# Seven directions in the projection, sums written over their products, and one more convolution direct

## What is computed

```python
for _ in range(3):                                   # x: 16 images, 64 channels, 64 x 64
    t = relu(conv3x3(x, w1) + b1)
    x = x + (conv3x3(t, w2) + b2) / 3
x = relu(x)
qkv = qkv_w @ x                                      # 8 heads, 8 values each, per pixel
k, v = ln(k), ln(v)                                  # w*(t-mean)/(std(ddof=1)+1e-5)+b, over the 8 values
kv = einsum('bhnd,bhne->bhde', k, v) / N             # 8 x 8 per head
ret = einsum('bhnd,bhde->bhne', q, kv) + x
out = gelu(o2_w @ gelu(o1_w @ ret) + x)
```

## Time and profile before

| | before |
|---|---|
| median of 3 runs | 1303.31 us (1300.70 to 1306.62) |
| the profiled execution | 1304.89 us, span 1303.10 us |
| TensorE busy (matmul) | 1188.0 us, 91% |
| VectorE busy | 1085.5 us, 83% |
| ScalarE busy | 597.4 us, 46% |
| mean granted clock of TensorE | 0.967 |

### The profile page before, as it was taken

The page is one execution under the profiler, slowest core; times in us unless marked ns, Lnnn a source line. Parts: engine busy times, 40 slices in busy tenths (PEclk is TensorE's granted clock), DMA queues, the critical chain, the costliest instruction groups (busy, mean ns, idle before and its releaser), DMA issues. The chain is left out here.

```text
span 1303.1 us, 40508 instructions
## 1 busy us (share of the span) xinstructions
PE 1188.0 (91%) x18613; PEld 805.4 (62%) x18613; DVE 1085.5 (83%) x1425; ACT 597.4 (46%) x642; POOL 91.1 (7%) x119
## 2 busy tenths in 40 slices
PE   6989999999999999999999999999999999785845
PEld 2546766577556766676566875676665875445432
DVE  3658888899888998899988997989978998987563
ACT  0212324454455626544455625554455625544573
POOL 2010110001010100101000100101000110110000
PEclk9989999999999999999999999999999999897876
DMA  7430330315061513515061422515061330430221
GB/s 131 91 68 1 69 68 2 68 36 102 18 150 33 102 36 99 101 36 102 2 164 35 86 52 70 129 35 102 2 163 36 69 69 34 100 68 2 82 51 65
DMA packets 87130, 88.95 MB, mean 68 GB/s; under 512 B 70320, under 2 KB 70320, under 8 KB 86960
## 3 DMA queue, kind: packets, MB, share of 16 engines
q0 software_dynamic: 13824, 51.91, 21.0%
q1 hardware_dynamic: 72496, 33.86, 10.3%
q10 hardware_dynamic: 640, 0.59, 0.3%
HBM read 17.66 MB, written 16.78 MB: 26 GB/s over the span
## 5 line engine op out<-in xcount | busy, mean ns | idle before, releaser
L956 PE MATMUL ps<-xs,w_t 64*64 64x512 f32 x4608 | 519.0, 594 | 10.2 <-DMA xs<-dx 6.3
L982 PE MATMUL ps<-v,fw 64*64 64x256 f32 x6912 | 398.9, 380 | 5.9 <-ACT m L552 4.1
L956 PEld LDWEIGHTS ps<-xs,w_t 64*64 64x64 f32 x4608 | 255.6, 134 | 224.1 <-issue 173.9
L982 PEld LDWEIGHTS ps<-v,fw 64*64 64x64 f32 x6912 | 302.2, 133 | 98.3 <-issue 18.4
L524 ACT ACTIVATE t<-ps,b_col 128x1024 f32<-128x1024 f32 x64 | 72.3, 1129 | 260.4 <-PE ps L956 204.9
L494 POOL DMA_DIRECT2D xs<-dx x96 | 83.4, 965 | 1154.3 <-DVE dx L829 1144.6
L722 DVE TENSOR_TENSOR q<-t 128x2112 f32<-128x2112 f32 x48 | 113.2, 2357 | 28.3 <-ACT t L524 15.4
L989 PE MATMUL ps<-v,sw 64*64 64x256 f32 x2304 | 134.4, 376 | 1.7 <-ACT t L524 1.7
L989 PEld LDWEIGHTS ps<-v,sw 64*64 64x64 f32 x2304 | 116.4, 132 | 21.5 <-issue 10.4
L554 ACT ACTIVATE m<-ps 128x1024 f32<-128x1024 f32 x80 | 82.2, 1028 | 65.6 <-PE ps L982 37.1
L836 DVE TENSOR_REDUCE rstd<-g 128x128 f32<-128x1024 f32 x64 | 77.1, 1216 | 38.7 <-ACT g L606 38.7
(11 more groups left out here) (108 smaller groups left out, 1115.4 us busy)
## 6 DMA issues: line engine op xcount, KB each, us to landing
xs<-dx POOLq DMA_DIRECT2D x96, 528.0 KB, 6.1
xs<-in_x SPq DMA_DIRECT2D x64, 256.0 KB, 5.1
out<-y SPq DMA_DIRECT2D x32, 512.0 KB, 3.1
q<-in_L_conv_w ACTq DMA_DIRECT2D x2, 144.0 KB, 6.1
v<-in_L_conv_w ACTq DMA_DIRECT2D x2, 144.0 KB, 7.3
b_col<-in_L_conv_b ACTq DMA_DIRECT2D x4, 0.2 KB, 6.1
y<-in_L_conv_qkv_w SPq DMA_DIRECT2D x4, 16.0 KB
y<-in_L_conv_o_w SPq DMA_DIRECT2D x4, 16.0 KB
```

The lines of the kernel that those rows point to most:

```text
L956: last = mm(to[CH * side:CH * side + CH, BANK * p:BANK * p + BANK], w1_t[half, tap, :], tile[half, rows, c:c + COLS], start=tap == 0, stop ...
L982: last = mm(to[CH * i:CH * i + CH, at:at + SPAN], fw[rows, product, c, :], from_t[rows, tiles, place, i, c:c + COLS], start=c == 0, stop=c ...
```

## The change

- **Merge.** `sums` is gone and `m` has two buffers, used in turn, with the products ordered so that the first of each couple lie together. VectorE adds the second to the first in place, waits for itself (`summed`), and makes -2 times the second plus the sum in place. The intermediate plane `first` and row 2 come next, then a wait for `halved`, `last` and row 1. ScalarE drains part 0 only after the merge of the half before the previous one.
- **Projection.** The eight values of a head, less their mean, lie in seven dimensions; `kvw` now holds seven orthonormal directions, 112 columns. Drains, squares and reductions handle 896 values where they handled 1024. The maps `k_affine` and `v_affine` turn back; that is more setup in `make_rest`.
- **Last pair.** Half 1 of step 2 of pair 7 is direct: 15 halves of L989 in place of 16.
- **Start.** Chunks are 9, 7, 9 and 7 rows; block 0 needs chunk 0, block 1 chunks 1 and 2, block 3 chunk 3. The first copy of w1 is loaded by SyncE, ahead of x.
- **Order.** All tables are written anew. In the gaps of an iteration, PROJECT 4 to 7 of pairs 0 to 5 move from 11, 14, 17, 19 to 10, 12, 14, 16, RELU 0 and 1 from 16 and 30 to 9 and 23; the merge of the old pair's half 0 of step 1 moves from 9 to 10, behind the new pair's second spread of step 0 (10 to 8); the merge of the new pair's second half moves from 18 to 16, behind PROJECT 7. In iteration 8, PROJECT 1 and 2 of pair 6 are behind gaps 10 and 12, PROJECT 3 behind 16, PROJECT 4 to 7 behind 22 to 26; the first spread of pair 7's last convolution is behind 25 (before: 30), DEVIATION 1 behind 28 (before: 26), OUTER 4 to 7 and the FOLDs behind 31 to 35, the second spread behind 36 (before: 37). In iteration 9, OUTER 0 comes ahead of PROJECT 5 and UP 3 ahead of DOWN 2, and RELU 0 comes behind DEVIATION 1.

```diff
-CHUNK_ROWS = 8
-CHUNKS = ROWS // 2 // CHUNK_ROWS
+CHUNK_ENDS = (0, 9, 16, 25, 32)
+CHUNKS = len(CHUNK_ENDS) - 1
...
-SHORT = ({(1, 1), (2, 1)}, {(1, 1), (2, 1)}, {(1, 1), (2, 1)})
+SHORT = ({(1, 1), (2, 1)}, {(1, 1), (2, 1)}, {(1, 1)})
...
-        m = sb("m", [P, 4, BANK])
+        m = [sb(f"m{k}", [P, 2, 2, BANK]) for k in range(2)]
         m_ends = [sb(f"m_ends{k}", [P, 2, BANK]) for k in range(2)]
-        sums = sb("sums", [P, 4, BANK])
...
+            sp.dma_start(w_raw[0][:, 0:CH * K * K], w1.rearrange("o c y x -> o (c y x)")).then_inc(w_in[0], 16)
             for c in range(CHUNKS):
                 load_chunk(0, c)
...
-                    if part == 0 and plane:
-
-                        act.wait_ge(sums_made, plane)
-                    to = m[:, 2 * part:2 * part + 2, :].rearrange("p k (s e) -> p k s e", s=2)
+                    if part == 0 and plane >= 2:
+
+                        act.wait_ge(*merged(plane - 2))
+                    to = m[plane % 2][:, :, part, :].rearrange("p k (s e) -> p k s e", s=2)
...
-                    nc.scalar.activation(kv[:, k % 4].rearrange("p i j t c -> p (i j t c)"), ring_ps[SLOT[a, *s]],
-                                         ACT.Copy)
+                    taken = ring_ps[SLOT[a, *s]].rearrange("p (i e) -> p i e", i=2)[:, :, 0:4 * FREE]
+                    nc.scalar.activation(
+                        kv[:, k % 4].rearrange("p i j t (h d) -> p i (j t h) d", d=HD)[:, :, :, 0:LAST_D],
+                        taken.rearrange("p i (g d) -> p i g d", d=LAST_D), ACT.Copy)
...
+                total, b_and_d = m[plane % 2][:, 0], m[plane % 2][:, 1]
                 dve.wait_ge(drained, NUMBER[unit])
-                vec.tensor_tensor(sums[:, 0:2, :], m[:, 0:4:2, :], m[:, 1:4:2, :], ALU.add)
-                vec.tensor_tensor(sums[:, 2:4, :], m[:, 0:4:2, :], m[:, 1:4:2, :], ALU.subtract
-                                  ).then_inc(sums_made, 1)
-                a_, c_, b_, d_ = (sums[:, k, :] for k in range(4))
+                vec.tensor_tensor(total, total, b_and_d, ALU.add).then_inc(summed, 1)
+                dve.wait_ge(summed, plane + 1)
+                vec.scalar_tensor_tensor(b_and_d, b_and_d, -2.0, total, ALU.mult, ALU.add).then_inc(halved, 1)
+                a_, c_ = (total[:, k, :] for k in range(2))
+                b_, d_ = (b_and_d[:, k, :] for k in range(2))
...
-                dve.wait_ge(sums_made, plane + 1)
-                for side in range(2):
-                    vec.scalar_tensor_tensor(rows_of(2)[:, side], tiles_of(c_)[:, side], 2.0, tiles_of(a_)[:, side],
-                                             ALU.mult, ALU.add)
-                vec.tensor_tensor(rows_of(1), tiles_of(b_), tiles_of(d_), ALU.add)
                 dve.wait_ge(v_made, made)
                 spare = eo.rearrange("p c r w -> p (c r w)")
                 first, last = spare[:, 0:BANK], spare[:, BANK:BOTH]
                 vec.scalar_tensor_tensor(first, c_, 0.5, a_, ALU.mult, ALU.add)
+                for side in range(2):
+                    vec.scalar_tensor_tensor(rows_of(2)[:, side], tiles_of(c_)[:, side], 2.0, tiles_of(a_)[:, side],
+                                             ALU.mult, ALU.add)
+                dve.wait_ge(halved, plane + 1)
                 vec.scalar_tensor_tensor(last, d_, 4.0, b_, ALU.mult, ALU.add).then_inc(ends_made, 1)
+                vec.tensor_tensor(rows_of(1), tiles_of(b_), tiles_of(d_), ALU.add)
...
-                        for c in ((0, 1), (2,), (3,), ())[b]:
+                        for c in ((0,), (1, 2), (), (3,))[b]:
...
-                            at = BANK * p + P * j
+                            at = BANK * p + FREE * j
...
-                                last = mm(ring_ps[SLOT[a, *s]][columns, at:at + P],
+                                last = mm(ring_ps[SLOT[a, *s]][columns, at:at + FREE],
```

More of the change, by code:

```diff
@@ L194 @@
+    (OUTER, 4): 24.05, (OUTER, 5): 24.3, (OUTER, 6): 24.41, (OUTER, 7): 27.79, (FOLD, 0): 28.23, (FOLD, 1): 29.37,
+    (FOLD, 2): 29.54, (FOLD, 3): 29.61, (UP, 0): 30.09, (UP, 1): 31.73, (FINISH, 0): 32.68, (DOWN, 0): 32.89,
+    (DOWN, 1): 33.91, (FINISH, 1): 34, (UP, 2): 34.52, (DOWN, 2): 36.33, (UP, 3): 37.16, (FINISH, 2): 37.36,
+    (FINISH, 3): 37.7, (DOWN, 3): 37.91,
 }
 LAST = {
-    (PIXELS, 0): -0.48, (PIXELS, 1): -0.38, (PROJECT, 0): 9.54, (PROJECT, 1): 11.73, (PROJECT, 2): 12.45,
-    (PIXELS, 2): 13.02, (PROJECT, 3): 14.43, (INVERT, 0): 15.69, (DEVIATION, 0): 17.11, (NORMALISE, 0): 17.26,
@@ L205 @@
-    (FOLD, 3): 36.85, (UP, 0): 37.47, (RELU, 1): 38.4, (DOWN, 0): 38.53, (UP, 1): 39.2, (FINISH, 0): 39.53,
-    (UP, 2): 40.28, (FINISH, 1): 41.23, (DOWN, 1): 41.28, (DOWN, 2): 41.61, (FINISH, 2): 41.9, (UP, 3): 41.9,
-    (FINISH, 3): 41.9, (DOWN, 3): 41.9,
+    (PIXELS, 0): 5.56, (PROJECT, 0): 9, (PROJECT, 1): 10.09, (PIXELS, 1): 11.41, (PROJECT, 2): 12.02,
+    (PROJECT, 3): 16.47, (INVERT, 0): 16.81, (DEVIATION, 0): 19.75, (NORMALISE, 0): 19.84, (NORMALISE, 1): 20.37,
+    (PIXELS, 2): 20.97, (OUTER, 0): 21.14, (OUTER, 1): 22.57, (PROJECT, 4): 22.65, (NORMALISE, 2): 23.42,
@@ new lines @@
+    (PROJECT, 5): 23.82, (PIXELS, 3): 24.61, (NORMALISE, 3): 25.12, (OUTER, 2): 25.51, (OUTER, 3): 25.78,
+    (PROJECT, 6): 25.93, (RELU, 0): 26.53, (PROJECT, 7): 26.82, (INVERT, 1): 28, (DEVIATION, 1): 28.48,
+    (NORMALISE, 4): 28.49, (OUTER, 4): 31.24, (NORMALISE, 5): 31.59, (OUTER, 5): 31.82, (NORMALISE, 6): 31.93,
+    (OUTER, 6): 33.18, (NORMALISE, 7): 33.57, (OUTER, 7): 33.92, (FOLD, 0): 33.94, (FOLD, 1): 33.94,
+    (RELU, 1): 34.19, (FOLD, 2): 34.76, (FOLD, 3): 35.7, (UP, 0): 36.9, (DOWN, 0): 37.41, (UP, 1): 38.35,
@@ new lines @@
+    (OUTER, 0): 56.77, (OUTER, 1): 56.86, (PROJECT, 5): 57.34, (OUTER, 2): 59, (OUTER, 3): 60.39,
+    (PROJECT, 6): 60.74, (PROJECT, 7): 63.03, (INVERT, 1): 63.69, (NORMALISE, 4): 63.84, (NORMALISE, 5): 63.84,
+    (DEVIATION, 1): 65.23, (RELU, 0): 65.58, (NORMALISE, 6): 65.95, (RELU, 1): 67.78, (OUTER, 4): 67.91,
+    (OUTER, 5): 68.62, (OUTER, 6): 70.03, (NORMALISE, 7): 70.29, (OUTER, 7): 70.31, (FOLD, 0): 73.5,
+    (FOLD, 1): 74.46, (FOLD, 2): 74.67, (FOLD, 3): 75.1, (UP, 0): 76.16, (UP, 1): 76.61, (FINISH, 0): 76.67,
```

135 lines of the change are left out of this document (67 added, 68 removed).

## The result

The changed kernel takes 1271.82 us (median of 4 runs, 1270.59 to 1272.49) against 1303.66 for the kernel before, measured beside it (4 runs): a ratio of 0.9755, 95% interval 0.9731 to 0.9778. It is 31.8 us faster where 22.1 were forecast. The profiled execution took 1272.30 us, its span 1270.6, 32.5 less than the span before.

The account below looks back on a forecast made before the run. TensorE was taken to bound the middle, VectorE 10% behind, and the chain through all engines the end. Terms -9.6 - 2.0 - 5 - 5.5 = -22.1 us gave 1281 us against the median of 1303.31, range 1269 to 1297.

Parts of the forecast that it names:

- Start: Up to the first convolution: fewer x rows for block 0 behind one w1 load give -2.0 us (0 to -3.3).
- a floor: At the start: transposes and copy of w1 end at about 10.5 us, the earliest the first convolution could start.
- Middle: Pairs 0 to 5: 0.8 columns, 0.6 DOWN wait, 0.2 buffer, 1.6 us a pair, in all -9.6 (0 to -16).
- The DOWN wait: In the middle: TensorE's 1.42 us wait hangs on VectorE's gapless run and shrinks by 0.6 or so (0 to 1.42).
- the 1 us forecast for the sums: On VectorE in the middle: summing in place saves one step of 0.12 us a merge, about 1 us a pair.
- Drains and reduction: Projections on ScalarE and VectorE: an eighth fewer elements, drains near 0.92 us, reduction near 1.08, seven-value runs costing nothing.
- End: Last pair's last convolution: direct half lets the first spread hide under block 3, second spread 3.8 earlier; -5 us (+2 to -7).
- Last attention: Last pair's attention: RELU 0 -1.8, OUTER 0 -0.9, drains -1.3, UP 3 -1.5; sum -5.5 us (0 to -8).
- Rival 2: Middle: columns don't set the projection and VectorE's run still ends late; 148.5 us a pair, 1290.6 us; chance 0.14.
- Rival 3: Middle: an `m` drain waits for a late merge, stopping TensorE; slower, 1315 us if 10.5 late; chance 0.06.
- Rival 1: End gives nothing back: chain over DEVIATION and FOLD arrives no earlier, attention's drains hit the same waits; 1291.5 us; chance 0.13.
- Rival 4: Helps more than counted: whole 1.42 wait and bank waits go, blocks start 3 earlier; about 1272 us; chance 0.15.

Follow-up runs that it names:

- e1: Changed kernel with both copies of w1 issued by ScalarE again, the x chunks of 9, 7, 9 and 7 rows kept: 1272.52 us, ratio 0.9765.
- e7: Changed kernel with the middle's tables of places (convolutions of pairs 0 to 6, attention of pairs 0 to 5) from the kernel before: 1282.13 us, ratio 0.9845.
- e2: Changed kernel with x loaded in chunks of eight rows again, block 0 waiting for two chunks, one w1 copy still on SyncE: 1274.66 us, ratio 0.9783.
- e11: Changed kernel with the old places before the last attention, but the last pair's first convolution direct and its first spread under block 3: 1298.23 us, ratio 0.9956.
- e4: Changed kernel with the projection's weights padded with zeros to 128 columns, drains still reading 112 of each 128: 1279.27 us, ratio 0.9812.
- e3: Changed kernel with part 0's drain waiting for both sums of the half before, as with one product buffer: 1275.92 us, ratio 0.9787.

## Why the prediction was right, and where not

The time lies in the range named, but 9 us below the forecast of 1281 and close to its lower end. Two misses in the same direction, -5.0 and -4.3, make that up; the terms of the sum that look met are partly luck, as told below.

- **Start: a term mis-sized, -7.0 for -2.0** (-6.2 at the first block, which is what was priced). The failing step is "the transposes and the copy of w1 end at about 10.5, a floor". It took w1's arrival as given and priced SyncE's new load only by what it delays. e1 shows the floor exactly where it was put (10.52) when w1 stays on ScalarE; the load on SyncE is what moves it, since w1 lands 3.0 to 3.7 us after its issue instead of 5.2 to 7.0. The -3.3 named as the best case was that of the chunks alone (13.77 to 10.52).
- **First long passage through products: a term not priced, -4.3.** The wait of 2.14 us stood in the trace of before, and the second buffer was priced only by the pair (0.2). The question not asked was what the longest single wait on `m` costs, and what the clock does behind it.
- **Middle: the sum right (1.6 for 1.59), its parts not.** The columns were 0.87 for 0.8; the proportional price was the right one. The DOWN wait gave 0 for 0.6: the failing step is that VectorE's run "has no gap". It has one, 0.45 us for a FOLD, and so the run begins behind TensorE. Buffer and order together gave 0.7 for 0.2: in the kernel before, 0.6 us more than in e7 lie between that OUTER and the product behind it, of which the profile calls only 0.25 a wait, and 0.2 more in the units that follow. Two errors cancelled, so the sum is right by luck.
- **VectorE's saving was there, and was lost.** Its busy time is 1.7 us a pair less (534.57 to 527.85 over four pairs), and 0.95 of what it saved is seen as the longer wait. That isn't a measurement of the 1 us forecast for the sums, since the FOLD it waits for came earlier too. The first step of a merge is still 1.25 us (1078.11 to 1079.36, as in the earlier trace rows).
- **Drains and reduction: right.** They take 0.92 and 1.08 us (0.919 and 1.080 mean), as put; the runs of seven values cost nothing.
- **End: -4.6 for -5, the number partly luck and the reason half right.** In the profiles of e1 and e2 the same term reads -7.2 and -8.1. The first spread does run under block 3 (1160.24), and the second is 4.6 earlier against pair 5's store, for the 3.8 worked out. But e11 shows that this isn't the direct half's doing alone; the prediction gave the order next to no part. TensorE's wait behind block 3 was not foreseen either (6.47 us; before it was 9.00 and 5.49).
- **Last attention: -5.9 for -5.5**, with the parts not measured one by one. From the second spread to the first UP it is 3.2, for the 4.0 put on RELU's place, OUTER's place and the shorter drains (the wait of 3.78 in the earlier trace rows is 2.82); from there to the end it is 2.6, for the 1.5 put on UP 3.
- **Rivals.** Rival 2 is out by e4. Rival 3 didn't occur: TensorE's waits of the middle have no `m` drain at all. Rival 1 is what e11 shows for the old order. Rival 4 named 1272, which is the time measured, and by luck: the 1.42, which was to go, stayed whole. Its other reasons were in part right: the waits for drains into `m` are gone (3.2 us in 5 places in the kernel before), and the last blocks start 1.6 earlier against pair 5's store.

## What to carry to other kernels

Before pricing an engine's saving on the path, look along its run for the smallest wait for the bounding engine: whatever is saved ahead of that wait is lost in it, however gapless the rest looks, and work added ahead of it is free only up to its length. A load that moves to another queue changes not only what it delays but which transfers run beside it, so price its own landing too. In a hand-set order the parts of a change are not additive: taking one part back within the other order costs more than the part ever gave.

## What the runs showed of the hardware

A wait of TensorE at the same place is followed by a lower clock in one execution and not in another, and the longer wait need not be the one. After a wait of 2.19 us block 0 of the last pair ran 9.69 us in the changed kernel, and after one of 3.64 us 8.01 in e1 (stretches of the changed kernel, then of e1):

```profile
1131.00:1141.00 10.00, 9.79 (x94) 3.77 (x98) 7.58 (x10) 2.91 (x4) 1.75 (x2) 0.83 0.58 110
```

```profile
1132.40:1140.50 8.10, 8.06 (x90) 3.54 (x94) 5.95 (x7) 1.58 (x3) 1.68 (x2) 1.00 0.72 136
```

So a wait away from the end of the chain can cost about its own length (2.26 us in e3, for 2.55 in all), or nearly twice that (2.14 in the kernel before, for 4.06); and in the end stage, where TensorE waits often, single executions differ by 3.6 us with the same code (190.9 to 194.5 from pair 5's store).
